# Two-layer graph network on one core: both attention rows copied by ScalarE, first squares inside the counting, and denominator rows moved

## The reference

```python
h = relu(layernorm(x))
HW = h @ W;  s = HW @ a[:512, 0];  t = HW @ a[512:, 0]
e = leaky_relu(s[src] + t[dst], 0.2)             # per edge
att = softmax of e over the edges of one src node
agg = segment_sum(att * h[dst], src)             # 1250 x 512
x = x + silu(agg) @ base_w.T + einsum('nip,oip->no', b_splines(agg), spline_w)
h = relu(layernorm(x))
x = x + three layers of: h = relu(batchnorm(normalized_adjacency @ (h @ W[l].T) + b[l]))
```

## Time and profile before

| what | value |
|---|---|
| runs | 612.61, 612.69, 613.86 us |
| profiled execution | 613.75 us, span 611.9 us |
| PE busy | 587.3 us (96%) |
| DVE busy | 435.6 us (71%) |
| ACT busy | 342.3 us (56%) |
| POOL busy | 35.4 us (6%) |
| chain that ended last | PE 71%, DVE 4%, ACT 4%, issue 2% of the span |
| mean granted TensorE clock | 0.986 of 2.4 GHz |

### The profile page before, as it was taken

The page is one execution under the profiler, slowest core; times in us unless marked ns, Lnnn a source line. Parts: engine busy times, 40 slices in busy tenths (PEclk is TensorE's granted clock), DMA queues, the critical chain, the costliest instruction groups (busy, mean ns, idle before and its releaser), DMA issues.

```text
span 611.9 us, 9806 instructions
## 1 busy us (share of the span) xinstructions
PE 587.3 (96%) x3951; PEld 364.2 (60%) x3951; DVE 435.6 (71%) x746; ACT 342.3 (56%) x450; POOL 35.4 (6%) x40
## 2 busy tenths in 40 slices
PE   6799899999999999999999999999999999999995
PEld 2567867555654555555555555687557855587552
DVE  7995999997669999995499779362374335552555
ACT  3887768677799989891798234044132333142112
POOL 1000430000000000000000030042000020000000
PEclk9789899999999999999999999999999999999998
DMA  9960500000510000000000000250200000000112
GB/s 308 344 249 2 217 1 1 2 2 1 193 46 1 0 2 1 1 1 1 0 2 1 0 1 2 80 203 1 69 2 0 1 2 0 2 1 0 43 43 84
DMA packets 11645, 29.18 MB, mean 48 GB/s; under 512 B 750, under 2 KB 2542, under 8 KB 11344
## 3 DMA queue, kind: packets, MB, share of 16 engines
q1 hardware_dynamic: 11600, 28.54, 12.6%
HBM read 22.71 MB, written 5.84 MB: 47 GB/s over the span
## 4 chain that ended last, share of the span: by engine, by line
PE 71%; DVE 4%; ACT 4%; issue 2%; DVEq 0%; ACTq 0%
PE bank L1914 32%; PE bank L1998 21%; PE bank L1955 13%; PE bank L1817 3%; DVE BHL L1318 1%; ACT kx L831 1%; DVE EXL L1219 1%; ACT kx L843 1%; ACT kx L842 1%; DVE AL L1226 0%; DVE WKh L1275 0%; ACT ks L853 0%; ACT kx L856 0%; ACT kx L836 0%; PE bank L1898 0%
## 5 line engine op out<-in xcount | busy, mean ns | idle before, releaser
L1914 PE MATMUL bank<-BHL,WKh 128*128 128x418 f16 x1152 | 204.8, 339 | 1.0 <-DVE BHL L1318 1.0
L1914 PEld LDWEIGHTS bank<-BHL,WKh 128*128 128x128 f16 x1152 | 111.1, 97 | 94.2 <-DVE BHL L1318 2.0
L1998 PE MATMUL bank<-C,YH 128*128 128x418 f16 x360 | 122.4, 340 | 0.0
L1998 PE MATMUL bank<-C,YL 128*128 128x418 f16 x360 | 122.3, 340 | 0.0
L1569 DVE SCALAR_TENSOR_TENSOR Z<-bank,yback,dvb 128x418 f32<-128x418 f32 x36 | 23.4, 651 | 52.1 <-PE bank L1998 52.1
L984 ACT ACTIVATE bnc<-bnm,tiny 128x1 f32<-128x1 f32 x12 | 3.5, 294 | 92.0 <-DVE bnm L1577 92.0
L1998 PEld LDWEIGHTS bank<-C,YH 128*128 128x128 f16 x360 | 35.3, 98 | 28.8 <-issue 0.8
L947 ACT ACTIVATE YH<-bank,dvl 128x512 f16<-128x512 f32 x30 | 20.5, 687 | 56.6 <-PE bank L1955 56.6
L1998 PEld LDWEIGHTS bank<-C,YL 128*128 128x128 f16 x360 | 35.2, 98 | 28.0
L1512 DVE SCALAR_TENSOR_TENSOR YL<-bank,dvl,YH 128x512 f16<-128x512 f32 x30 | 22.0, 749 | 38.9 <-ACT YH L947 38.9
L1955 PE MATMUL bank<-GWH,XH 128*128 128x512 f32 x120 | 47.6, 396 | 0.0
(11 more groups left out here) (249 smaller groups left out, 986.4 us busy)
## 6 DMA issues: line engine op xcount, KB each, us to landing
WKf<-in_wk SPq DMA_DIRECT2D x9, 1024.0 KB, 6.6
c_scratch<-C SPq DMA_DIRECT2D x1, 3200.0 KB, 11.1
C<-c_scratch SPq DMA_DIRECT2D x1, 3200.0 KB, 9.9
GWf<-in_gwT SPq DMA_DIRECT2D x3, 1024.0 KB, 11.0
XT<-in_xT SPq DMA_DIRECT2D x1, 2500.0 KB, 8.8
outT<-Z SPq DMA_DIRECT2D x3, 625.0 KB, 3.1
Wt<-in_WT SPq DMA_DIRECT2D x1, 1024.0 KB, 6.9
hx<-in_x SPq DMA_DIRECT2D x1, 1024.0 KB
```

Source lines behind the costliest of these rows:

```text
L1914: ins = mm(bank[:, 4 * (g % 2) + o, 0:G], lhs, rhs, start=(u == 0 and q == 0 and i == 0), stop=(u == UNITS - 1 and q == PAIR - 1 and i == 2))
L1998: ins = mm(bank[:, u % YB, 0:G], Y[:, j, o * P:(o + 1) * P], C16[:, j, g * G:(g + 1) * G], start=(j == 0 and i == 0), stop=(j == NT - 1 an ...
```

## The change

SQUARES_AHEAD goes from 2 to 4, with block 0 taken out of the row: it is multiplied behind group n = 6 of the counting, into its own 128 columns of bank 0. VectorE reads it at n = 8, and row spread 3, which writes the same columns, waits for that read. Blocks 1 and 2 come right behind `degrees`, ahead of the last two lots; block 3 behind the lots; blocks 4 and 5 behind the spreads. ScalarE copies both rows; `second_rows` is gone. The two partial sums of squares are added. `denominator_row(0)` moves from behind the sums of n = 15 to n = 14, ahead of `weight_scale`; at n = 22 and 23 `denominators(1)` and `denominator_row(1)` come ahead of `weights_low`.

```diff
--- before.py
+++ after.py
@@ -72,7 +72,9 @@
 YB = 4
 SQUARE_BLOCKS = KB
 SQUARES_READ = 3
-SQUARES_AHEAD = 2
+SQUARES_FILL = 3
+SQUARES_AHEAD = 4
+SQUARES_EARLY_AT, SQUARES_EARLY_READ = 6, 8
 SQUARES_IN = (0, 1, 2)
 DV_SETS = ((0, 4), (4, 8), (8, NT))
 DV_AT = (3, 5, 6)
@@ -370,6 +372,8 @@
         h_low = sem("h_low")
         mask_set = sem("mask_set")
         mask_late = sem("mask_late")
+        sq_early = sem("sq_early")
+        sq_early_read = sem("sq_early_read")
         masked = sem("masked")
         pq_spread = sem("pq_spread")
         pq_cols = sem("pq_cols")
@@ -765,8 +769,11 @@
 
             def attention_rows(i):
                 t0, t1 = SETS[i]
-                act.wait_ge(pq_spread, 1 if i == 0 else 3)
-                for k in range(1 if i == 0 else 2):
+                if i == 1:
+                    act.wait_ge(pq_spread, 3)
+                for k in range(2):
+                    if i == 0:
+                        act.wait_ge(pq_spread, k + 1)
                     c0 = rows_at(i, k)
                     ins = nc.scalar.copy(PQ[:, k, t0 * P:t1 * P], flat_bank[:, c0:c0 + (t1 - t0) * P])
                 ins.then_inc(pq_set, 1)
@@ -1085,6 +1092,13 @@
                 V.tensor_tensor_reduce(out=JSD[:, :], in0=ident[:, :], in1=bank[:, 3, 0:P], scale=1.0, scalar=0.0,
                                        op0=ALU.mult, op1=ALU.add, accum_out=wss[:, 0:1]).then_inc(sq_read, 1)
 
+            def early_squares():
+                dve.wait_ge(sq_early, 1)
+                dve.wait_ge(st_done, 3)
+                V.tensor_tensor_reduce(out=jrise[:, 0:4, :], in0=ident[:, :].rearrange("p (a b) -> p a b", a=4),
+                                       in1=bank[:, 0, 3 * P:4 * P].rearrange("p (a b) -> p a b", a=4), scale=1.0,
+                                       scalar=0.0, op0=ALU.mult, op1=ALU.add, accum_out=wss[:, 1:2]).then_inc(sq_early_read, 1)
+
             def order_check():
                 V.tensor_tensor(drise[:, :, :], dT[:, :, 1:FINE + 1], dT[:, :, 0:FINE], ALU.subtract)
                 V.tensor_tensor(rises[0:1, :], first16[0:1, 1:STRIPS + 1], first16[0:1, 0:STRIPS], ALU.subtract)
@@ -1121,6 +1135,8 @@
                     order_check()
                 if n == ORDER_FLAG:
                     order_flag()
+                if n == SQUARES_EARLY_READ:
+                    early_squares()
                 if n in SCALES_AT:
                     row_scales(SCALES_AT[n], *BATCHES[SCALES_AT[n]])
 
@@ -1333,14 +1349,6 @@
                     ins = V.scalar_tensor_tensor(xc, bank[:, 4 * (g % 2) + c, 0:G], wsc[:, 1:2], xc, ALU.mult, ALU.add)
                 ins.then_inc(kan_copied, 1)
 
-            def second_rows():
-                t0, t1 = SETS[0]
-                c0 = rows_at(0, 1)
-                dve.wait_ge(pq_spread, 2)
-                V.tensor_copy(PQ[:, 1, t0 * P:t1 * P], flat_bank[:, c0:c0 + (t1 - t0) * P]).then_inc(q_set, 1)
-                dve.wait_ge(q_set, 1)
-
-            second_rows()
             attention_sum(0)
             attention_sum(1)
             attention_f32(0)
@@ -1362,24 +1370,25 @@
                     block_squares()
                 if n == 9:
                     dve.wait_ge(sq_read, 1)
-                    V.tensor_copy(wsc[:, 0:1], wss[:, 0:1]).then_inc(sumsq_set, 1)
+                    V.tensor_tensor(wsc[:, 0:1], wss[:, 0:1], wss[:, 1:2], ALU.add).then_inc(sumsq_set, 1)
                 if n == 13:
                     denominators(0)
                 if n == 14:
+                    denominator_row(0)
                     weight_scale()
                 if n == 15:
-                    denominator_row(0)
                     aggregated(0, 0)
                     aggregated(0, 1)
                 if n == 16:
                     aggregated(0, 2)
                     aggregated(0, 3)
-                if FIRST_HALF < n <= FIRST_HALF + LOOP_LOWS:
-                    weights_low(n - FIRST_HALF - 1)
                 if n == 22:
                     denominators(1)
                 if n == 23:
                     denominator_row(1)
+                if FIRST_HALF < n <= FIRST_HALF + LOOP_LOWS:
+                    weights_low(n - FIRST_HALF - 1)
+                if n == 23:
                     aggregated(1, 0)
                 if n == 24:
                     aggregated(1, 1)
@@ -1652,10 +1661,13 @@
             def block_squares(i):
                 pe.wait_ge(wk_in(i), wk_count(i))
                 top = WKf[:, i, :].bitcast(BF16).rearrange("p (n k) -> p n k", k=2)[:, :, 1]
+                out = bank[:, 0, 3 * P:4 * P] if i == 0 else bank[:, 3, 0:P]
                 for q in range(BLK // P):
                     part = top[:, q * P:(q + 1) * P]
-                    ins = mm(bank[:, 3, 0:P], part, part, start=(i == 0 and q == 0),
-                             stop=(i == SQUARE_BLOCKS - 1 and q == BLK // P - 1))
+                    ins = mm(out, part, part, start=(i <= 1 and q == 0),
+                             stop=(i in (0, SQUARE_BLOCKS - 1) and q == BLK // P - 1))
+                if i == 0:
+                    ins.then_inc(sq_early, 1)
                 if i == SQUARE_BLOCKS - 1:
                     ins.then_inc(sq_done, 1)
 
@@ -1717,6 +1729,8 @@
                         turn(t)
                 for t in range(NT):
                     if n == TURN_AT[t] + 2:
+                        if n == SQUARES_EARLY_READ + 1:
+                            pe.wait_ge(sq_early_read, 1)
                         row_spread(t)
                 if n == VTURN_AT:
                     vectors_turned()
@@ -1732,6 +1746,8 @@
                 for t in range(NT):
                     if n == TURN_AT[t] + 1:
                         dots(t)
+                if n == SQUARES_EARLY_AT:
+                    block_squares(0)
 
             pe.wait_ge(ctl_set, 1)
             bad = pe.value_load(ctl[0:1, 0:1], min_val=0, max_val=1 << 20)
@@ -1797,10 +1813,12 @@
                 spread(3, dvc, t0, t1).then_inc(dv_spread, 1)
 
             degrees()
+            for i in range(1, SQUARES_FILL):
+                block_squares(i)
             for k in range(EARLY_LOTS + 2, ALL_LOTS):
                 pe.wait_ge(ct_set, k - 1 - V_LOTS)
                 lot_turned(k)
-            for i in range(SQUARES_AHEAD):
+            for i in range(SQUARES_FILL, SQUARES_AHEAD):
                 block_squares(i)
             pe.wait_ge(degs_out, 1)
             rows_spread(0)
```

## The result

The changed kernel takes 611.75 us in the median of 10 runs (611.27 to 612.56), the kernel before 612.66 (612.46 to 613.89, 10 runs). The ratio is 0.9983, 95% interval [0.9975, 0.9990]: 1.0 us faster, give or take half a microsecond. The forecast was 612.3, in a range of 611.1 to 613.6; the change lies within the 0.2% that I called no difference (611.46 was its lower edge), close to that edge. The profiled execution took 611.78 us, 1.97 less than the profiled one before, whose time had been 1.1 above its kernel's median.

A forecast was written before the change was run, and what follows sets the result against it. Bound by when the third attention group starts, TensorE or VectorE, whichever is later. From the profiled execution, 613.75 - 1.05 (counting) - 0.59 (attention start) - 0.87 (rows) + 1.07 (clock under spreads) = 612.31, taken as 612.3; range 611.1 to 613.6 us.

The forecast's parts named there:

- The start of the attention, 0.59: Before the attention: with ScalarE copying the second row, VectorE's first sum comes 0.59 us earlier; bounds 0.3 and 0.66.
- The rows, 0.87 together: Third attention group starts 0.87 us earlier from both denominator-row moves, VectorE's row being the later limit; bounds 0.5 and 1.3.
- the scale of 108.57 + 0.15 = 108.72 comes at 109.70: Second attention group: the first row's move delays VectorE's weight scale, so TensorE's start loses 0.73 us.
- DVE about 0.4 worse: First denominator row ahead of the weight scale: VectorE ends about 0.4 us worse, TensorE 0.25 worse.
- The counting, 1.05: Early squares behind the seventh group (n = 6) bring a gain of about 1.05 us; bounds 0 and 1.4.
- What filling the gap gives is the clock: Counting, seventh group: squares in TensorE's 1.01 us gap could stop the clock falling, gaining about 1.05 us.
- VectorE's reader, nothing: Counting: VectorE's 0.29 us read of the early block costs nothing, its waits being met or harmless.
- 1.4 us of cover: Counting: VectorE's one-hots behind the reader wait 1.4 us for TensorE, so the reader delays nothing.
- The clock under the spreads, 1.07: Row spreads before the attention: the clock falls 0.9 us into them, losing 1.07 us; bounds 0 and 2.0.
- Rival 1: Before the row spreads the clock holds, so the 1.07 us loss is absent: 611.2 us; chance 0.20.

The follow-up runs named there:

- no_squares: The changed kernel with every move of squares undone, the other moves kept; median 611.49 us, ratio 0.9976 to the kernel before.
- fill_only: The changed kernel with block 0 of squares taken out of the counting and put with 1 and 2 behind `degrees`; median 613.35 us, ratio 1.0001 to before.
- squares_only: The kernel before with only the squares moved, with their reader and the sum of the two parts; median 614.27 us, ratio 1.0018.
- row0_back: The changed kernel with denominator_row(0) put back to n = 15, behind weight_scale; median 611.38 us, ratio 0.9979 to the kernel before.
- rows_only: The kernel before with only VectorE's order changed, both denominator-row moves; median 611.63 us, ratio 0.9983.
- fill_one: As no_squares_scale_first, with one block of squares put behind `degrees`; median 611.24 us, ratio 0.9973 to the kernel before.
- scale_first: The changed kernel with weight_scale ahead of denominator_row(0), both still at n = 14; median 610.98 us, ratio 0.9972 to the kernel before.
- no_squares_scale_first: The changed kernel with every move of squares undone and weight_scale ahead of denominator_row(0); median 611.54 us, ratio 0.9970 to the kernel before.
- after_shift: The changed kernel with eight one-column memsets added at VectorE's very start; median 612.41 us, ratio 0.9989 to the kernel before.

## Why the prediction was right, step by step

The time lay in the range and on the side forecast, but the terms behind it were not all right; two large ones cancelled.

1. *The start of the attention, 0.59.* Measured 3.60 - 2.98 = 0.62, in each of five profiles of kernels with both the copies and the changed squares. Right, and by the steps given: 0.3 from the copies alone, 0.3 from earlier spreads.

2. *The rows, 0.87 together.* Measured 28.54 - 27.38 = 1.16, within the bounds of 0.5 to 1.3. That VectorE's row, and not TensorE, sets the third group's start was right. The term was mis-sized at one step: "the scale of 108.57 + 0.15 = 108.72 comes at 109.70" carried along a wait of 0.44 us inside the scale's chain that belongs to no instruction there. It stood at 107.65 before, at the second of the small steps:

```profile
107.06 0.15 DVE L1240 TENSOR_SCALAR wsc<-bank 128x1 f32<-128x1 f32 x1
...
107.65 0.15 DVE L1242 TENSOR_SCALAR wsi<-wsc 128x1 int32<-128x1 int32 x1 [0.44 <-issue]
```

In the changed kernel it is gone from there, so TensorE's second group starts 0.52 late instead of 0.73, and VectorE's second row comes 0.4 earlier than I had it. From its low part ahead of the first row's spread to the second row's copy VectorE takes 26.61 us instead of 27.79: one split less (1.20), the wait for issue gone (0.44), the wait for the spread new (0.47). Where the wait for issue is still in the chain behind a row copied first (no_squares, fill_only) the second group starts 3.34 to 3.35 behind the row's spread, 0.35 later. And the two moves have different signs. The prediction had the first at "DVE about 0.4 worse" and VectorE as the later of the two engines; together that says that the first move costs 0.4, which the sum for both hid. squares_only, row0_back and the changed kernel differ there by one move each, with the wait for issue gone from all three: 28.18, 26.95, 27.38. The second row's move gives 1.23, the first row's costs 0.43, and the wait's going from the scale gives the 0.36 from 28.54 to 28.18.

3. *The counting, 1.05.* The step that failed is "What filling the gap gives is the clock", taken from one execution for all. In the state of the clock that the first profile had, it holds (1.2). In the state with the clock up at 23.5 to 24 the gap isn't there and it is a loss of 1.4; with the clock up near 29, nothing to a loss of 0.4. The prediction did see that the median might not have the full gain, but had no row for a loss. Over all executions the moved squares lose alone (1.0018), and next to the other parts they are worth nothing that I could tell (0.9983 against 0.9976 without them).

4. *VectorE's reader, nothing.* Wrong in an unforeseen way: in all seven profiles of kernels with it the masks come 0.4 us later, by a wait for issue. In the same seven it is gone from the scale (step 2), so part of the loss comes back there: 0.36 us in squares_only. The reader's 0.29 us and, with the clock up early, its wait for the third row spread (1.25 us in row0_back) also bring VectorE's one-hots of the tenth group late, by 0.31 to 0.46 us in five of the seven, where I had counted on 1.4 us of cover. That cover was itself made by the lower clock at 36 to 38 us: in rows_only, where the clock is up there, the one-hots are ready at 36.30 + 0.48 = 36.78 and the count starts at 36.90.

5. *The clock under the spreads, 1.07.* In the changed kernel 0: six profiles of kernels with its squares, all 2.02 us. Rival 1's case, which had a chance of 0.20, though not by its reason. The clock did fall, but ahead of the spreads, and was back at 66.2 to 68.2 us in all six. The gap was 1.16 us, not 1.8, as squares and lots ran at the lower clock. The mechanism is real: 3.33 and 2.60 us in fill_one and no_squares, a price of 1.3 and 0.6, within the bounds of 0 to 2.0. The page that the prediction names for this term, TensorE: Matmul & The Clock Gate of the Trainium skill, section "HAM oscillation — how this bites in real kernels", tells of waits for DMA of 3 to 5 us; the gaps here were 1.0 to 1.8 us, so it was no support for the term at this size.

The sum of what the two first profiles show: `degrees` starts 0.61 earlier (60.33 for 60.94), the masks take 0.39 more, the start 0.62 less, the rows 1.16 less: 2.00, the 2.01 by which the third group starts earlier. Of this, the masks' loss and the last two showed in every profile of a kernel with the parts in question: 0.62 + 1.16 - 0.39 = 1.39 of gain. The medians differ by 0.9, so over all executions the counting gave back about 0.5 (an estimate from these numbers). That the forecast of 612.3 lay within 0.6 of 611.75 is in part luck: the -1.05 for the counting and the +1.07 for the spreads were both absent on the whole, and a loss of 0.39 that I hadn't seen stood against 0.29 more from the rows.

The Trainium skill, TensorE: Matmul & The Clock Gate, section "What's actually happening", says that the ramp to full speed varies by run: one and the same kernel has more or fewer of its first matmuls at the lower clock. The trace agrees, for the return after the first fall: the clock was back at 25.2 and at 29.7 us in two executions of the changed kernel, and between 23.5 and 35.2 in kernels whose first 20 us are alike.

**What is open.** Why VectorE's wait of 0.4 us and TensorE's of 0.7 to 1.0 stand where they do: they move when code ahead of them or the program's layout changes, and the profile names no releaser. I took them for loads of instructions, and the traces bear that out, though no run tested it. They hold the DMA packets of kind instruction with their times (before: 32 on q8, of 16 KB, and 13 on q14). One q14 packet of 8 KB starts 0.5 to 0.8 us behind the end of each of VectorE's thirteen waits (1.2 in scale_first), and moves with the wait from one kernel to the other; in rows_only it starts 0.84 us ahead of the row copy, for which VectorE waits anyway. A q8 packet starts 2.7 to 3.3 us ahead of `degrees` in the eleven kernels where that runs through, and only 0.6 to 0.7 ahead in the three where it is broken. Other q14 packets have no wait near them, and which engine a packet serves the trace doesn't say. How often each state of the clock occurs was not measured either: the profiles are fourteen executions, and the clock came up at 23.5 to 23.8 in five of them, at 24.9 to 25.2 in three, at 27.9 to 29.7 in four, and was up until 28.3 or 28.4 in two.

**Better than both.** no_squares_scale_first (0.9970), scale_first (0.9972) and fill_one (0.9973) are each 1.7 to 1.8 us faster than before and 0.6 to 0.8 faster than the changed kernel by the ratios, though their intervals reach into its own. Of these, no_squares_scale_first is the simplest: it needs no early block, no reader and no second PSUM place. row0_back's order without the squares wasn't tried.

## What to carry to other kernels

Where an engine's order is written out by hand, ask of each step which other engine is waiting for it: a copy of 0.6 us moved ahead of a 1.3 us split gave 1.2 us, the same copy moved to where its row was not yet spread made the engine wait 0.47 us and cost 0.4. Ask too which engine sets the next start: what the other one saves is worth nothing. Filler work put into a gap is free only at the clock, and in the order, at which it was costed: price it at both clocks, and look at what stands behind it in the queue. Before a term of a microsecond is taken from one profile, look at a second execution of the same kernel; where the runs fall into two groups a microsecond apart, the profile shows only one of them.

## What the runs showed that I had not expected

The clock can fall behind a stretch in which TensorE was never idle: it did so at 63.8 us in the changed kernel, 4.3 us after its last idle time (0.30 us), behind 16 transposes, 100 matmuls of one column (60.33 to 62.97) and the first squares. It was low somewhere between 61 and 70 us in every profile of every kernel here, whether the gap behind `degrees` was filled or not.

A wait for issue of 0.4 us on VectorE stood in the weight scale in six profiles, at the masks in six, one instruction ahead of them in after_shift, and nowhere that the profile shows in rows_only. It comes on top of the 0.48 us that VectorE takes at the branch behind the counting in all of them. In three kernels whose TensorE code in that place is the same or nearly so as before, `degrees` was broken by a wait of 0.74 to 1.02 us that before doesn't have.
